# Feeding the first attention block's projections into the feed-forward block before it, and scoring heads in pairs

## What is computed

```python
x = x + 0.5 * _L1_ffn_ref(_layernorm(x, axis=-1), L1_ffn_wg, L1_ffn_w1, L1_ffn_w2)
x = x + _L1_attn_ref(_layernorm(x, axis=-1), L1_attn_w_dkv, L1_attn_w_q, L1_attn_w_uk, L1_attn_w_uv, L1_attn_w_o)

# _L1_attn_ref, 16 heads of 16 features
c_kv = hidden_states @ w_dkv.T
q = (hidden_states @ w_q.T).reshape(B, S, HEADS, HEAD_DIM)
k = (c_kv @ w_uk.T).reshape(B, S, HEADS, HEAD_DIM)
v = (c_kv @ w_uv.T).reshape(B, S, HEADS, HEAD_DIM)
scores = jnp.einsum('bqhd,bkhd->bhqk', q, k) * scale
scores = scores + alibi_bias(S)[None, None]
attn = jax.nn.softmax(scores, axis=-1)
out = jnp.einsum('bhqk,bkhd->bqhd', attn, v).reshape(B, S, HIDDEN)
return out @ w_o.T
```

## Time and profile before

| what | us |
|---|---|
| median of 3 runs | 588.79 |
| their range | 585.11 to 592.06 |
| the profiled execution | 585.49 |
| its span, first to last instruction | 583.8 |
| PE busy | 514.1 (88%) |
| DVE busy | 414.0 (71%) |
| ACT busy | 253.0 (43%) |
| POOL busy | 127.2 (22%) |

### The profile page before, as it was taken

How to read it: one execution, slowest core, us unless ns; L and a number is a source line. 1 busy time by engine, 2 the same in 40 slices (tenths; PEclk the granted TensorE clock), 3 DMA queues, 4 the chain that set the end, 5 groups by cost and what they waited for, 6 DMA issues and landing times.

```text
span 583.8 us, 9241 instructions
## 1 busy us (share of the span) xinstructions
PE 514.1 (88%) x3106; PEld 436.4 (75%) x3106; DVE 414.0 (71%) x1227; ACT 253.0 (43%) x544; POOL 127.2 (22%) x192
## 2 busy tenths in 40 slices
PE   1999999999968999999999977898267989879995
PEld 1888888888846888888888867777256767658884
DVE  3669896597885436675587778997565878847985
ACT  3646644453222224433353362372244767534341
POOL 1001000010020001000010064264232555414351
PEclk9999999999975999999999997998678999999998
DMA  6323201100000000000000002400832622000011
...
DMA packets 16718, 24.83 MB, mean 43 GB/s; under 512 B 2720, under 2 KB 11168, under 8 KB 16576
## 3 DMA queue, kind: packets, MB, share of 16 engines
...
...
## 4 chain that ended last, share of the span: by engine, by line
PE 70%; DVE 12%; issue 8%; ACT 4%; POOL 4%; DMA 1%; ACTq 1%; DVEq 0%; POOLq 0%
PE ps L556 21%; PE ps L558 19%; PE ps L557 19%; DVE gel L1372 1%; PE ps L566 1%; PE ps L869 1%; POOL al L487 1%; DVE ps L1635 1%; DVE z L1294 1%; PE ps L841 1%; PE ps L829 1%; DMA post_b<-in_posts_dram 1%; DVE gel L1370 1%; PE ps L855 1%; PE ps L941 1%
## 5 line engine op out<-in xcount | busy, mean ns | idle before, releaser
L556 PE MATMUL ps<-zh,w0u_h 128*128 128x512 f32 x256 | 102.7, 401 | 2.5 <-issue 2.5
L558 PE MATMUL ps<-zl,w0u_h 128*128 128x512 f32 x256 | 102.2, 399 | 0.0
L557 PE MATMUL ps<-zh,w0u_l 128*128 128x512 f32 x256 | 101.8, 398 | 0.0
L998 ACT ACTIVATE gel<-ps 128x512 f32<-128x512 f32 x64 | 38.2, 597 | 105.1 <-PE ps L558 105.0
L1390 DVE TENSOR_TENSOR act<-gel,ps 128x512 f32<-128x512 f32 x64 | 43.9, 685 | 53.4 <-ACT gel L998 53.3
L556 PE MATMUL ps<-w0d_h,ah 128*128 128x256 f32 x256 | 73.3, 286 | 1.2 <-DVE al L1397 1.0
L557 PE MATMUL ps<-w0d_h,al 128*128 128x256 f32 x256 | 72.4, 283 | 0.0
L558 PE MATMUL ps<-w0d_l,ah 128*128 128x256 f32 x256 | 72.4, 283 | 0.0
L1397 DVE TENSOR_TENSOR al<-act,ah 128x512 fp32r<-128x512 f32 x64 | 43.9, 687 | 23.5 <-ACT ah L1004 23.2
L487 POOL TENSOR_TENSOR al<-act,ah 128x512 fp32r<-128x512 f32 x32 | 42.2, 1319 | 84.7 <-ACT ah L1072 84.2
L1004 ACT ACTIVATE ah<-act 128x512 fp32r<-128x512 f32 x64 | 40.3, 630 | 41.5 <-DVE act L1390 41.5
...
## 6 DMA issues: line engine op xcount, KB each, us to landing
...
```

The source lines that it names most:

```text
L556: pe.matmul(o, lh, rh, start=start, stop=False, **kw)
L557: pe.matmul(o, ll, rh, start=False, stop=False, **kw)
L558: return pe.matmul(o, lh, rl, start=False, stop=stop, **kw)
L998: nc.scalar.activation(gel[:, n % 2, :], ps[:, 2 * (n % 2), :], ACT.Gelu_apprx_tanh).then_inc(gelu_s, 1)
```

## The change

1. **Block 0's projections move into `ffn1`.** z of block 0 is prepared at c = 2 and 3 of `ffn1`'s block 1 (`prepare_at`, with the new test `feeds`). Its two half transposes, c, q, k and v are issued by PE between the experts of c = 3 to 7, all in one bank (`feed_bank(0)`, bank 3), so that each waits for the copies of the one before. z's halves lie in `qs`, k's in `ks`.
2. **The loads and clears they need come earlier.** SP waits for the last `ffn0` output on PE instead of for `x`; ACT copies the weights at c = 4 of block 0, POOL splits them at c = 6 and 7 of block 0 and c = 0 and 1 of block 1, clears `shift` at c = 5 of block 0 and `va` at c = 3 of block 1. The second half of the constant rows of `ks` (`k_rows(1)`) is copied at the start of `attn1`.
3. **Scores by pairs.** PE scores a pair of heads at even steps: 256 columns into `EARLY_BANK` (7), then 512 columns into bank 0 or 1. Each has a semaphore of its own. DVE makes the same four bias instructions for a pair. The bank of the attention's outputs is now `MISC_BANK`, the one of block 1's projections.
4. **`scores_t` stands ahead of `scores` in each step.**
5. **Block 1's projections stand later**, and block 1's accumulation and layernorm are in the first steps on DVE:

```diff
-Z_HALVES = (5, 7)
-C_STEP = 9
-Q_STEPS = (11, 15)
-K_STEPS = (13, 17)
-V_STEPS = (27, 44)
+Z_HALVES = (8, 10)
+C_STEP = 12
+Q_STEPS = (14, 20)
+K_STEPS = (16, 18)
+V_STEPS = (25, 41)
...
+        def feeds(st, b):
+
+            return st.kind == "ffn1" and b == 1 and st.after == "attn1"
+
         def prepare_at(st, b):
 
-            return 5 if b == 0 else 4
+            return 5 if b == 0 else 2 if feeds(st, b) else 4
...
             if "attn1" in stages:
-                for b in range(2):
-                    sp.wait_ge(x_s[b], last_ffn0 + 1)
+                sp.wait_ge(down_s, U0 * f0)
                 sp.dma_start(wa_raw, wa).then_inc(wa_s, 16)
...
+                    if b == 0 and c == 5:
+                        nc.gpsimd.memset(shift[:, :, :, :], 0.0).then_inc(shz_s, 1)
+                        pool.wait_ge(shz_s, 1)
+                        nc.gpsimd.memset(shift[:, :, :, ONE_COL:ONE_COL + 1], 1.0).then_inc(shz_s, 1)
+                    if (b, c) in ((0, 6), (0, 7), (1, 0), (1, 1)):
...
+                    if b == 1 and c == 3:
+                        pool.wait_ge(wal_s, WL)
+                        nc.gpsimd.memset(va[:, :, :, :], 0.0).then_inc(wal_s, 1)
...
                         mm.then_inc(h1_s, 1)
                         if c == 1:
                             logits(3, routed["ffn1", fb])
+                        if feeds(st, b):
+                            if c == 4:
+                                half_transposes(st.p + 2, 1)
+                            if c == 5:
+                                project_q(0, 0)
+                            if c == 6:
+                                project_k(0, 1)
+                            if c == 7:
+                                project_v(0)
                         if c >= LAG:
                             down1(n - LAG)
+                        if feeds(st, b):
+                            if c == 3:
+                                pe.wait_ge(tk, TK * routed["ffn1", fb] + 1)
+                                half_transposes(st.p + 2, 0)
+                            if c == 4:
+                                pe.wait_ge(wal_s, WL)
+                                split_ready(st.p + 2)
+                                project_c(0)
+                            if c == 5:
+                                project_k(0, 0)
+                            if c == 6:
+                                project_q(0, 1)
+                            if c == 7:
+                                project_v(1)
...
                 for s in range(4 * HEADS + SUM):
-                    if s < 4 * HEADS:
-                        scores(s)
                     if s % GROUP == 1 and GROUP < s < 4 * HEADS + GROUP:
                         shift_turn(s // GROUP - 1)
                     if TURN <= s < 4 * HEADS + TURN:
                         scores_t(s - TURN)
+                    if s < 4 * HEADS and s % 2 == 0:
+                        scores(s // 2)
...
+                if gp == 0:
+                    pe.wait_ge(acc_s, E * f0 + U1 * blocks_before_attn1 - 1)
+                else:
+                    pe.wait_ge(sm0_s, gp)
+                pe.matmul(ps[:, EARLY_BANK, 0:2 * P], qs[0:K_ROWS, slot, 0:P], ks[0:K_ROWS, slot, :, 0:P],
+                          start=True, stop=True).then_inc(s0_ps, 1)
+                if gp >= 2:
+                    pe.wait_ge(sm1_s, gp - 1)
+                pe.matmul(ps[:, gp % 2, :], qs[0:K_ROWS, slot, P:SEQ], ks[0:K_ROWS, slot, :, :],
+                          start=True, stop=True).then_inc(s1_ps, 1)
...
                 for s in range(4 * HEADS + SUM):
-                    if s < 4 * HEADS:
-                        bias_min(s)
-                    if s % GROUP == GROUP - 1 and s < 4 * HEADS:
-                        shift_hi(s // GROUP)
-                        shift_lo(s // GROUP)
+                    if s < 4 * HEADS and s % 2 == 0:
+                        bias_min(s // 2)
+                        if s % GROUP == 2:
+                            shift_hi(s // GROUP)
+                            shift_lo(s // GROUP)
+                    if s == 0:
+                        left_acc(st, 0, 1)
+                    if s == 2 or s == 4:
+                        prepare(p + 1, s // 2 - 1)
```

276 lines of the change are left out of this document (138 added, 138 removed).

## The result

| | before | after |
|---|---|---|
| runs beside one another | 4, median 590.42 us (585.11 to 596.26) | 4, median 603.64 us (599.34 to 608.29) |
| ratio | 1 | 1.0256, 95% interval 1.0132 to 1.0380 |
| profiled execution, span, mean granted clock | 585.49, 583.8, 0.953 | 605.02, 602.4, 0.928 |

The change makes the kernel slower, by about 15 us by the ratio (2.56% of 590) and 13.2 us by the medians, where +6.5 was forecast. Ratios here compare the runs of both kernels that lie within 1.5% of their kernel's fastest; medians are over all runs.

A forecast was written before the change was run, and what follows sets the result against it. Bounds: the wait for the first stacks, DVE ahead of it, and in the steps PE closely followed by DVE. Terms 1.3 - 1.1 + 5.3 + 1.0 + 0 = +6.5 us gave 595.3 us on the median, range 580 to 604.

The forecast's parts named there:

- POOL's moved work: Block 0 of ffn1: a clear and a wa_l piece beside DVE's four z instructions add 2.0 us, between 0 and +2.3.
- Routing: Routing on DVE: its last four small instructions may each wait for POOL's al or wa_l, +0.9 us, 0 to +4.4.
- First score: Start of attn1: the first stack lands at 420.1 us, so the first score comes 1.3 us later, between -6 and +5.
- Chain from z: From block 0's z in ffn1: seven projection pieces through one bank take 19.5 us, ending at 411.9; before, 15.8.
- through HBM: Block 0's first stack: from the last low part through HBM to its landing takes 8.2 us.
- Steps 0 to 20: Early attention steps: sums among first biases, copies at odd steps, earlier scores_t and pairs give -1.1 us, between -5 and +4.
- Second block's stack: Around step 26: block 1's stack lands late and PE waits, +5.3 us (0 to +7), plus +1.0 for the slow clock.
- Steps 27 to 75: Late steps: pairs save 6 to 8 us, waits for shift_out and out_lo cost as much; 0, between -8 and +12.
- The step's rate is PE's: Rival for the steps: PE's own work sets the pace, so pairs and earlier probs give 581.3 us; chance 0.23.
- Second stacks are hidden: Rival at steps 21 to 26: the 5.3 us wait for block 1's stack vanishes, leaving +1.2, 590.0 us; chance 0.22.
- DVE becomes the bound: Rival behind step 27: a pair's four biases hold up PE, 0.8 us in each of 10 groups, +14.5, 603.3 us; chance 0.15.
- Its own signs: Right: z ends about 392 us, first stack's rounding at 420. Wrong: z before 389, 32 steps under 36 or over 46 us.

The follow-up runs named there:

- e10: Changed kernel with scores ahead of scores_t, block 1's projections early, last sums ahead of the first bias, clear of va later: 593.5 us.
- e1: Changed kernel with the scores put ahead of the shift's turn and scores_t again: 597.0 us, ratio 1.0199 to the kernel before.
- e11: Kernel before with block 0's projections moved into ffn1 alone, and v projected at steps 25 and 41: 599.6 us, ratio 1.0238.
- e3: Changed kernel with block 0's projections, and the loads, clears and copies they need, back at their old places: 594.4 us, ratio 1.0107.
- e4: Changed kernel with ACT copying v ahead of the rounding of q in the step behind its projection: 599.2 us, ratio 1.0259.
- e2: Changed kernel with scores, bias and minimum per head again, one head each step: 606.3 us, ratio 1.0358 to the kernel before.
- e5: Kernel before with the paired scores alone, and v projected at steps 25 and 41: 589.4 us, ratio 1.0076.
- e12: Kernel before with 36 extra matmuls, results unused, in PE's wait ahead of the first score: 591.4 us, ratio 1.0047.
- the 111 runs: Runs of the unchanged kernel before, beside the experiments: 580 to 600 us, 4.6 us more for every 0.01 less mean granted clock.

## Why the prediction was wrong

The sign was right, and 603.6 lies within 580 to 604, at its very edge; the size was off by more than the terms allowed. By its own steps:

- **POOL's moved work, +2.0 on z:** in block 0 z took 4.80 instead of 3.36 (+1.44). Right in kind. For the attention's z "z runs from 388.7, ready at 392.4": it ran at 389.48 to 393.4. Right.
- **Routing, +0.9 of 0 to +4.4:** the step that failed first. It cost 3.2 us (`eq`), since three of four short instructions ran into one of POOL's laid back to back. I had laid the durations side by side as if held instructions kept their places; the rows show that a held `eq` ends just after POOL has started its next, so the next `eq` meets that one, until POOL's row ends. First score +3.0 and first turn +2.7, forecast +1.3. PE waited 9.1 us for z, forecast 8.
- **Chain from z, 19.5 us; through HBM, 8.2:** 20.5 (393.4 to 413.9) and 7.95 (413.9 to 421.85). Right.
- **Steps 0 to 20, -1.1:** measured +5.9 between the turns of 5 and 21. This is the largest miss, and the term that failed is the clock, put at nothing here: PE's idle time grew by 0.2 us (7.3 to 7.5), its busy time by 5.7 (23.1 to 28.8), at 0.66 instead of 0.89, and from 430 to 440 us at 0.50 where before had 0.99. The sums among the first biases do hold others up (POOL's `zs_e` waits 6.45 us for them, with the rounding of pair 4 queued behind it), but with the sums put first the stretch still took 32.8 us (e10), against 33.5 with the order alone undone (e1). With the move alone it took 36.0 (e11), with the projections back at their old place 30.7 (e3). So the move brings most of the loss; through which of its waits the clock fell stays open.
- **Second block's stack, +5.3 and +1.0 for the clock:** ACT waited for `k_raw`, 2.55 us and not about 5, and PE's `out_back` for the copy of v behind it, 3.62 us, as described; the stretch from 21 to 29 lost 4.7, and PE's idle time there grew by 4.8. e4 took 3.0 off by moving that copy. Mechanism right, size right within a microsecond or two, but added to steps that were late anyway.
- **Steps 27 to 75, 0:** between -8 and +12 the value was +4.1 from the turn of 29 to that of 65, and +1.2 more to the end. Both forces were there and both were mis-sized. Pairs, forecast to save 6 to 8 us, saved 4.4 with `scores_t` first (56.2 in e2, 51.8 after) and 0.2 with the order of before (47.6, 47.4 in e5). The order, forecast at up to 7, cost 8 to 10 without pairs and 3 to 6 with them, though the waits for `shift_out` were 0.45 us in some groups, not 0.65 in all. The wait for `al` was forecast at +1.0 and measured +0.75 to +0.95. What was missing is what such a wait can do to the clock behind it, 2.2 us a dip by e12.
- **The rivals.** "The step's rate is PE's": refuted; pairs alone were 0.8% slower by the ratio and 2.3 us better at equal clock, not 14 us faster. "Second stacks are hidden": refuted by the wait at 475.42. "DVE becomes the bound": not as a rate of all groups, but at one place, the second output's low part; +14.5 was close to the result for the wrong reasons.
- **Its own signs:** z ended at 393.4 and the first stack's rounding began at 421.85, near the 392 and 420 given. 32 steps "over 46 us" was a sign of being wrong: those from 21 to 53 took 47.7, those from 29 to 61 46.0.

The common error: I priced the clock as +1.0 in one place. The line of the 111 runs puts the changed kernel's lower clock (0.930 against 0.947) at 7.8 us, about what the sum lacks of the 15, though part of that clock lies in waits that are counted already. That 603.6 lies within the range at all owes as much to its width as to the sum.
